# A mixture-of-experts router without the search for ties, and three ScalarE constants as immediates, in an audio tower on one core

## The chip, the core and the metric

The kernel runs on one core of a Trainium2 chip. A core has TensorE (PE: matmuls, and PEld, its weight loads), VectorE (DVE), ScalarE (ACT), GpSimd (POOL) and SyncE (SP, which issues DMAs). Each engine works through its own list of instructions in order, and the engines wait for each other by semaphores. The metric is device time in microseconds. Three runs of the kernel before took 646.54 us in the median (645.55 to 648.94).

## The reference

The input is x, 128 sequences of 375 steps and 64 features. Three layers follow one another:

```python
for i in range(3):                        # selective state-space layers
    delta = softplus(x @ W_dbc[0] * W_dt + b_dt);  B, C = x @ W_dbc[1:]
    h[t] = exp(delta * A) * h[t-1] + delta * x * B;  y = sum(h * C) + D * x
    if i < 2: x = mean of neighbouring steps of y      # 375 -> 187 -> 93
h = h + attention(layernorm(h))           # 8 heads, normalized q and k, y = 0.5(q.k)^2 + q.k + 1
h = h + experts(layernorm(h))

# experts: 6 experts, the two best of each token are mixed
rh = relu(f @ router_w1 + b1)
expert_logits = softmax(rh @ router_w2 + b2)
top_w, top_i = top_k(expert_logits, 2)    # of equal values the lower index is taken
routing_weights = softmax(top_w)
expert_out = relu(relu(f @ w1 + b1) @ w2 + b2) @ w3 + b3      # all six
out = sum over the two chosen of routing_weights * expert_out
```

The change concerns `top_k` and `routing_weights`: for each token six probabilities, of which the greatest and the second are found, with weights 1/(1+e) and e/(1+e), where e is exp(second - first).

## The kernel before

The 128 sequences are worked in 16 groups of 8 (`NG = 16`, `GB = 8`). A group passes four state-space units (A and B: the halves of the first layer; C, D: the second and third), then `att` and `ffn`. Each of these is cut into steps, such as `A.z`, `att.pm30` or `ffn.top`. Which engine does a step is fixed, and the order in which an engine does the steps of all groups is written out by hand in the table `ORDER` (one list for each engine; PE's entries also name the PSUM bank). Units of some four groups are thus in work at once. A step waits through `need(g, ...)` for the steps that it depends on, through `need(..., back=1)` for readers of a buffer in the group before.

The names that matter here:

- `att.pm` (ACT, L1057): eight times a group, squares the attention scores out of PSUM with the bias 2 (tile `two_col`), 93x744 each. PE's `y` (L1366) reads them.
- `lnv` (ACT, L1021): logarithm of a layer norm's variance plus a small constant (`eps_col`), once in `att` and once in `ffn`; `rnorm` (ACT, L1047): an exponential with the bias `ln_col`.
- the router, once a group: PE's `ffn.lg` makes the logits, 93x48 (8 sequences x 6 experts) in PSUM. DVE's `route1` (L1800, L1801: `mx`, `shift`) subtracts the greatest. ACT's `prexp` (L1082) takes the exponential. DVE's `ffn.top` (L1805 to L1816) is twelve small steps, each waiting for the one before: the sum, its reciprocal, a search for the first expert at the maximum with the help of `rank` (which settles ties), the probabilities without it, their maximum, the same search again, and `diff`, the difference of the two best. ACT's `topexp`, `topln`, `toprec` (L1086, L1090, L1094) turn `diff` into weights.
- `ffn.split` (POOL, L919 to L933): seven steps that make the gates from the two one-hot masks `oh0`, `oh1` and cut them into three bf16 parts. PE's `gT` (L1449) transposes these when the last part, `lo`, is there; ACT's `gateT` (L1112) copies them out and PE's `g_0` to `g_2` (L1422) spread them.
- `du` (L889), `y` (L893, L896), `qe` (L911) and others are POOL's further work.
- `hidw0` to `hidw2`, `fin` (DVE, L1821, L1825), PE's `o` (L1461) and `oT` (L1468), ACT's `out` (L1120, tile `osb`) end a group. `osb` is single: each `out` waits for the store of the group before.
- `prep.flags` and `prep.again` (DVE, L1584 to L1590, L1556) with PE's `prep.flag` (L1197) between them test, after the last state-space unit, whether the whole work must be done over by a general path (`GENERAL`), which does not happen with these inputs.

## Time and profile before

| | |
|---|---|
| median of three runs | 646.54 us (645.55 to 648.94) |
| span of the profiled execution | 644.8 us; its own time is not listed apart; the runs lie 0.8 to 4.1 us above the span |
| PE, DVE, ACT, POOL busy | 572.2, 540.6, 525.0, 423.5 us |
| granted clock of TensorE, mean | 0.983 |

The page gives busy time by engine, the chain of work that ended last, and groups of equal instructions with their mean duration and the idle time ahead of them. A line number is a line of the kernel; `pm<-ring,two_col` reads: writes tile `pm`, reads `ring` (PSUM) and `two_col`. "<-" behind an idle time names what ended it.

### The profile page before, as it was taken

How to read it: one execution, taken by the hardware profiler on the slowest of the kernel's cores; microseconds unless marked ns; L12 is line 12 of the kernel's file. 1: busy time of each engine (PE TensorE's matmuls, PEld its weight loads, DVE VectorE, ACT ScalarE, POOL GpSimd, SP SyncE). 2: the span in 40 equal slices, each digit the busy share in tenths (PEclk: the TensorE clock that was granted, in tenths of full speed). 3: DMA queues.
4: the chain of work that ended last, by engine and by line, in shares of the span. 5: the costliest groups of instructions: out<-in, count | busy, mean ns of one | idle time of the engine just before them, and what ended most of it. 6: DMA issues, size and time to landing. Idle time of an engine off the chain costs nothing.

```text
span 644.8 us, 22886 instructions
## 1 busy us (share of the span) xinstructions
PE 572.2 (89%) x9531; PEld 302.5 (47%) x9531; DVE 540.6 (84%) x1019; ACT 525.0 (81%) x1044; POOL 423.5 (66%) x549
## 2 busy tenths in 40 slices
PE   3777778999999999999999999999999999999972
PEld 2333234545455555455445455455545545545431
DVE  5898999999899899989898999999898987764441
ACT  1345668989899999998898998999999888888761
POOL 7758899788867677768567766767686755423110
PEclk9998879999999999999999999999999999999998
DMA  3432222221220213230211212220221001000001
GB/s 78 83 82 63 65 59 59 61 52 31 52 48 20 56 43 77 47 74 14 69 31 45 55 44 61 58 47 15 68 49 29 5 8 31 17 14 14 2 14 29
DMA packets 77575, 28.52 MB, mean 44 GB/s; under 512 B 69271, under 2 KB 77463, under 8 KB 77463
## 3 DMA queue, kind: packets, MB, share of 16 engines
q1 hardware_dynamic: 71290, 25.92, 17.6%
q10 hardware_dynamic: 6173, 1.05, 0.9%
q8 instruction: 77, 1.26, 0.9%
q14 instruction: 35, 0.29, 0.1%
HBM read 13.25 MB, written 3.05 MB: 25 GB/s over the span
## 4 chain that ended last, share of the span: by engine, by line
PE 44%; ACT 19%; DVE 17%; POOL 9%; issue 5%; DMA 2%; ACTq 2%; SPq 1%; POOLq 0%; DVEq 0%
PE ring L1274 7%; PE ring L1353 5%; ACT pm L1057 5%; PE ring L1366 4%; PE ring L1461 4%; DVE ring L1714 3%; PE ring L1260 3%; PE ring L1432 2%; PE ring L1441 2%; ACT hid L1100 2%; PE ring L1229 2%; PE ring L1249 2%; PE ring L1336 1%; PE ring L1412 1%; DVE carry_C L1710 1%
## 5 line engine op out<-in xcount | busy, mean ns | idle before, releaser
L1057 ACT ACTIVATE pm<-ring,two_col 93x744 f32<-93x744 f32 x128 | 107.4, 873 | 10.0 <-PE ring L1353 9.0
L1353 PE MATMUL ring<-q_exp,qk 32*93 32x372 f32 x512 | 56.4, 507 | 7.7 <-ACT ln_rows_a L1021 1.1
L1821 DVE TENSOR_TENSOR hidw<-hid,ring 128x744 f32<-128x744 f32 x48 | 44.3, 922 | 19.1 <-PE ring L1422 11.5
L911 POOL TENSOR_TENSOR q_exp<-qk,mask_q 128x1488 f32<-128x1488 f32 x16 | 42.9, 2683 | 22.2 <-DVE qk L1772 22.2
L1366 PE MATMUL ring<-pm,v 97*32 97x93 f32 x2048 | 53.7, 245 | 1.2 <-ACT pm L1057 0.4
L1100 ACT ACTIVATE hid<-ring,b_col 128x372 f32<-128x372 f32 x96 | 49.3, 568 | 1.5 <-PE ring L1441 0.9
L1366 PEld LDWEIGHTS ring<-pm,v 97*32 97x32 f32 x2048 | 42.4, 109 | 15.3 <-ACT pm L1057 3.4
L1107 ACT ACTIVATE hid<-ring,b_col 128x744 f32<-128x744 f32 x48 | 42.2, 879 | 8.9 <-PE ring L1432 6.4
L1432 PE MATMUL ring<-hid,w 64*64 64x372 f32 x384 | 40.3, 489 | 3.2 <-ACT hid L1100 2.7
L896 POOL TENSOR_TENSOR base_C<-base_C,carry_C 128x744 f32<-128x744 f32 x16 | 28.5, 1781 | 20.1 <-DVE carry_C L1723 9.5
L1441 PE MATMUL ring<-nrm_f,w 64*64 64x372 f32 x384 | 40.0, 486 | 0.2
L896 POOL TENSOR_TENSOR base_A<-base_A,carry_A 128x744 f32<-128x744 f32 x16 | 28.4, 1772 | 13.0 <-DVE carry_A L1723 12.9
L1461 PE MATMUL ring<-hidw,w 128*64 128x372 f32 x192 | 33.5, 484 | 0.0
L889 POOL TENSOR_TENSOR du_B<-delta_B,x_B 128x744 f32<-128x744 f32 x16 | 28.6, 1790 | 7.2 <-ACT delta_B L998 6.5
L889 POOL TENSOR_TENSOR du_A<-delta_A,x_A 128x744 f32<-128x744 f32 x16 | 28.6, 1788 | 5.3 <-ACT delta_A L998 5.2
L889 POOL TENSOR_TENSOR du_C<-delta_C,x_C 128x744 f32<-128x744 f32 x16 | 28.8, 1798 | 4.4 <-ACT delta_C L998 4.3
L1353 PEld LDWEIGHTS ring<-q_exp,qk 32*93 32x93 f32 x512 | 17.4, 154 | 25.8 <-POOL q_exp L911 2.8
L889 POOL TENSOR_TENSOR du_D<-delta_D,x_D 128x372 f32<-128x372 f32 x16 | 14.7, 917 | 21.4 <-ACT delta_D L998 17.8
L896 POOL TENSOR_TENSOR base_B<-base_B,carry_B 128x744 f32<-128x744 f32 x16 | 28.3, 1772 | 0.0
L1710 DVE TENSOR_TENSOR_SCAN carry_B<-dec_B,ring 128x744 f32<-128x744 f32 x16 | 27.2, 1698 | 0.3
L1710 DVE TENSOR_TENSOR_SCAN carry_A<-dec_A,ring 128x744 f32<-128x744 f32 x16 | 27.2, 1697 | 0.2
L1710 DVE TENSOR_TENSOR_SCAN carry_C<-dec_C,ring 128x744 f32<-128x744 f32 x16 | 27.1, 1694 | 0.1
(368 smaller groups left out, 1755.4 us busy)
## 6 DMA issues: line engine op xcount, KB each, us to landing
xin_A<-in_x_dram SPq DMA_DIRECT2D x62, 93.0 KB
xin_B<-in_x_dram SPq DMA_DIRECT2D x62, 93.0 KB
x_A<-x_A SPq DMA_DIRECT2D x32, 93.0 KB, 2.4
x_B<-x_B SPq DMA_DIRECT2D x32, 93.0 KB, 2.2
x_C<-x_C SPq DMA_DIRECT2D x32, 93.0 KB, 2.2
out_dram<-osb SPq DMA_DIRECT2D x15, 186.0 KB
x_D<-x_D SPq DMA_DIRECT2D x32, 46.5 KB, 2.2
w<-in_L_ffn_expert_w_dram SPq DMA_DIRECT2D x6, 48.0 KB
```

The lines of the kernel that those rows point to most:

```text
L889: g.tensor_tensor(halves(du[u][:]), halves(delta[u][:]), xs[u][:, 0::2, :], ALU.mult).then_inc(me, 1)
L896: g.tensor_tensor(base[u][:], base[u][:], carry[u][:], ALU.add).then_inc(me, 1)
L1057: a.activation(pm[q % 2][h][0:TOUT].rearrange("m a j n -> m a (j n)"), out_of(f"att.s{q}{h}", g)[0:TOUT, :, 0:COLS], ACT.Square, bias=two_ ...
L1100: ins = a.activation(hid1[:, h], out_of(f"ffn.h1_{k}", g)[:, h, 0:COLS], ACT.Relu, bias=b1_col[:, h, k:k + 1])
L1274: ins = mm(o[to:to + E, b, 0:wide], w[r:r + E, r:r + E], src[r:r + E, b, :], start=True, stop=True, tile_position=(r, to))
L1353: ins = mm(o[h][0:TOUT, b, 0:COLS], qk[r:r + 32, 1, q * TOUT:(q + 1) * TOUT], q_exp[r:r + 32, q].rearrange("p j n -> p (j n)"), start=True ...
L1366: ins = mm(o[32 * j:32 * j + 32, 0, h * TOUT:h * TOUT + TOUT], rows[:, at:at + 32], pm[q % 2][h][:, b, j, :], start=(b == 0), stop=(b == 1 ...
L1432: ins = mm(o[to:to + E, h, 0:COLS], w2[r:r + E, k, h], hid1[r:r + E, h], start=True, stop=True, tile_position=(r, to))
L1441: ins = mm(o[E * i:E * i + E, h, 0:COLS], w1[E * h:E * h + E, 2 * k + i], hn[E * h:E * h + E, :], start=True, stop=True, tile_position=(E ...
L1461: ins = mm(o[E * h:E * h + E, 0, 0:COLS], w3[:, k], hidw[k][:, h], start=False, stop=True, skip_group_check=True, tile_position=(0, E * h))
L1710: v.tensor_tensor_scan(carry[u][:], dec[u][:], b_made(u, g), 0.0, ALU.mult, ALU.add).then_inc(me, 1)
L1821: tt(hidw[k][:], hid2[:], out_of(f"ffn.g_{k}", g)[:, :, 0:COLS], ALU.mult).then_inc(me, 1)
```

## The change

- The bias columns `two_col`, `ln_col` and `eps_col` go; `pm`, `rnorm` and `lnv` take the numbers as immediates.
- `ffn.top` has six steps for the 16 groups of the main path: `sum`, `rest` (probabilities of the experts below the maximum), `rsum`, `m1`, `diff`, `oh1`. A tie now marks more than one expert in a mask.
- The first mask, `oh0`, is made by POOL in a new step `ffn.first`, which stands directly ahead of `ffn.split` in each group. Behind the split POOL adds both masks (`both`) and sums them up (`ties`) over the groups.
- Logits, probabilities and the reciprocal lie in SBUF (`logit`, `prob`, `st`) and no longer in the logits' PSUM bank, which `shift` frees in place of `diff`.
- The flag steps stand nearly last, behind `hidw1` of group 15, and also test the sum of ties. The general path keeps the search for ties.
- PE's, DVE's and POOL's lists are else the same, and ACT's and SP's are so wholly. A marker `!` that PE's list may carry is used by no entry.

On DVE, the router of group 0 before (`ring` is PSUM, `st` the small statistics, `oh` the masks):

```order
L1805 TENSOR_REDUCE st<-ring 93x8
L1806 RECIPROCAL ring<-st 93x8
L1807 SCALAR_TENSOR_TENSOR ring<-ring,rank 93x48
L1808 TENSOR_REDUCE st<-ring 93x8
L1809 TENSOR_TENSOR oh<-ring,st 93x48
L1810 SCALAR_TENSOR_TENSOR ring<-oh,ring 93x48
L1811 TENSOR_REDUCE st<-ring 93x8
L1812 TENSOR_TENSOR ring<-ring,st 93x48
L1813 TENSOR_TENSOR ring<-ring,rank 93x48
L1814 TENSOR_REDUCE st<-ring 93x8
L1815 TENSOR_TENSOR oh<-ring,st 93x48
L1816 SCALAR_TENSOR_TENSOR st<-st,ring 93x8
```

and with the change, from `mx` on, with the one foreign step (`quad_D`) that stands between `shift` and `sum` in both:

```order
L1803 TENSOR_REDUCE st<-ring 93x8
L1805 TENSOR_TENSOR logit<-ring,st 93x48
L1697 TENSOR_TENSOR quad_D<-ring,x_D 128x372
L1808 TENSOR_REDUCE st<-prob 93x8
L1810 SCALAR_TENSOR_TENSOR rest<-logit,prob 93x48
L1817 RECIPROCAL st<-st 93x8
L1819 TENSOR_REDUCE st<-rest 93x8
L1822 SCALAR_TENSOR_TENSOR st<-st 93x8
L1825 TENSOR_TENSOR oh<-rest,st 93x48
```

Twelve steps became six, and `diff` stands before the last mask. On POOL, the split of group 0 before, with the instruction ahead of it and the one behind:

```order
L885 TENSOR_TENSOR rows_three_A<-rows_left_A,rows_hi_A 128x186
L919 TENSOR_TENSOR gate<-oh,st 93x48
L921 TENSOR_TENSOR gate_rest<-oh,gate 93x48
L923 TENSOR_TENSOR gate<-gate_rest,st 93x48
L928 CAST gate_part<-gate 93x8x18
L930 TENSOR_TENSOR gate_part<-gate,gate_part 93x8x18
L931 TENSOR_TENSOR gate_rest<-gate,gate_part 93x48
L933 TENSOR_TENSOR gate_part<-gate_rest,gate_part 93x8x18
L889 TENSOR_TENSOR du_C<-delta_C,x_C 128x744
```

and with the change:

```order
L861 TENSOR_TENSOR rows_three_A<-rows_left_A,rows_hi_A 128x186
L896 TENSOR_SCALAR oh<-logit 93x48
L902 TENSOR_TENSOR gate<-oh,st 93x48
L904 TENSOR_TENSOR gate_rest<-oh,gate 93x48
L906 TENSOR_TENSOR gate<-gate_rest,st 93x48
L911 CAST gate_part<-gate 93x8x18
L913 TENSOR_TENSOR gate_part<-gate,gate_part 93x8x18
L914 TENSOR_TENSOR gate_rest<-gate,gate_part 93x48
L916 TENSOR_TENSOR gate_part<-gate_rest,gate_part 93x8x18
L917 TENSOR_TENSOR both<-oh 93x48
L919 TENSOR_TENSOR ties<-ties,both 93x48
L865 TENSOR_TENSOR du_C<-delta_C,x_C 128x744
```

One instruction came in front, two behind. On DVE, the flag steps before, between the `hidw1` of group 12 and `nrm_a` of group 15:

```order
L1821 TENSOR_TENSOR hidw<-hid,ring 128x744 x2
L1584 TENSOR_SCALAR ends<-least,decay_max 128x1 x4
L1586 TENSOR_SCALAR ends<-most 128x4
L1588 TENSOR_SCALAR ends<-ends 128x8
L1590 TENSOR_REDUCE flag_sum<-ends 128x1
L1683 MEMSET tick 1x1
L1556 TENSOR_SCALAR flag_i<-ring 1x1
L1683 MEMSET tick 1x1
L1759 TENSOR_TENSOR nrm_a<-ring,h_in 128x4x93
```

and with the change, at the end of the list, between `hidw1` and `hidw2` of group 15 (the last `fin` follows):

```order
L1837 TENSOR_TENSOR hidw<-hid,ring 128x744 x2
L1573 TENSOR_SCALAR ends<-least,decay_max 128x1 x4
L1575 TENSOR_SCALAR ends<-most 128x4
L1577 TENSOR_SCALAR ends<-ends 128x8
L1579 TENSOR_REDUCE flag_sum<-ends 128x1
L1581 TENSOR_REDUCE tie_sum<-ties 93x1
L1583 TENSOR_SCALAR tie_sum<-tie_sum 93x1
L1585 TENSOR_TENSOR flag_sum<-flag_sum,tie_sum 93x1
L1678 MEMSET tick 1x1
L1545 TENSOR_SCALAR flag_i<-ring 1x1
L1678 MEMSET tick 1x1
L1837 TENSOR_TENSOR hidw<-hid,ring 128x744
```

Three steps are new, and the wait of `flag_i` for PE now stands ahead of the last `hidw`. The diff, cut to its core (of `ORDER`, only the entries named above moved):

```diff
@@ -576,8 +552,8 @@
         PARTS = {"dve ffn.route1": ["mx", "shift"],
-                 "dve ffn.top": ["sum", "rsum", "key0", "kmax0", "oh0", "rest", "m1", "eq1", "key1", "kmax1", "oh1", "diff"],
-                 "pool ffn.split": ["w1", "w", "gate", "hi", "mid", "rest", "lo"]}
+                 "dve ffn.top": ["sum", "rest", "rsum", "m1", "diff", "oh1"],
+                 "pool ffn.split": ["w1", "w", "gate", "hi", "mid", "rest", "lo", "both", "ties"]}
         PARTS |= {f"pool {u}.three": ["left", "mid", "three"] for u in UNITS}
@@ -699,11 +677,9 @@
-        def router(g, k):
-
-            n_at = 64 * ("lg", "pr", "key", "rsum").index(k)
-            o_ = out_of("ffn.lg", g)[0:TOUT, 0]
-            return o_[:, n_at:n_at + GB] if k == "rsum" else o_[:, n_at:n_at + GB * NX].rearrange("m (b e) -> m b e", e=NX)
+        def logits_made(g):
+
+            return out_of("ffn.lg", g)[0:TOUT, 0, 0:GB * NX].rearrange("m (b e) -> m b e", e=NX)
@@ -913,11 +889,18 @@
             def experts(g_, u, s):
+                if s == "first":
+                    need(g_, "dve ffn.shift")
+                    need(g_, "pool ffn.ties", back=1)
+                    if g_ < NG:
+                        g.tensor_scalar(oh0[:], logit[:], 0.0, None, ALU.is_ge).then_inc(me, 1)
+                    else:
+                        g.memset(tick_pool[:, 0:1], 0.0).then_inc(me, 1)
                 if s == "split":
...
                     g.tensor_tensor(gate[:], oh1[:], st[:, 6, :, None].broadcast_to([TOUT, GB, NX]), ALU.mult).then_inc(me, 1)
-                    need(g_, "pool ffn.w1")
+                    need(g_, "pool ffn.w1", "pool ffn.first")
                     g.tensor_tensor(gate_rest[:], oh0[:], gate[:], ALU.add).then_inc(me, 1)
@@ -931,6 +914,9 @@
                     g.tensor_tensor(part[2], gate_rest[:][:, :, None, :].broadcast_to(wide), part[1], ALU.subtract).then_inc(me, 1)
+                    g.tensor_tensor(both[:], oh0[:], oh1[:], ALU.add).then_inc(me, 1)
+                    need(g_, "pool ffn.both")
+                    g.tensor_tensor(ties[:], ties[:], both[:], ALU.add).then_inc(me, 1)
@@ -1018,7 +1004,7 @@
                     need(g, f"pe {u}.rs", back=1)
-                    a.activation(ln_rows[w][:], out_of(f"{u}.var", g)[:, 0, 0:TOUT], ACT.Ln, bias=eps_col[:]).then_inc(me, 1)
+                    a.activation(ln_rows[w][:], out_of(f"{u}.var", g)[:, 0, 0:TOUT], ACT.Ln, bias=LN_EPS).then_inc(me, 1)
                 if s == "rstd":
@@ -1044,7 +1030,7 @@
                     need(g, "act att.lnorm")
-                    a.activation(qk_norm[:], qk_norm[:], ACT.Exp, bias=ln_col[:], scale=-0.5).then_inc(me, 1)
+                    a.activation(qk_norm[:], qk_norm[:], ACT.Exp, bias=12.0 * LN2, scale=-0.5).then_inc(me, 1)
                 if s == "v1":
@@ -1056,7 +1042,7 @@
                                  out_of(f"att.s{q}{h}", g)[0:TOUT, :, 0:COLS], ACT.Square,
-                                 bias=two_col[0:TOUT], scale=0.5 ** 0.5).then_inc(me, 1)
+                                 bias=2.0, scale=0.5 ** 0.5).then_inc(me, 1)
                 if s[:2] == "yT":
@@ -1078,8 +1064,8 @@
                     need(g, "dve ffn.shift")
-                    lg, pr = (router(g, k) for k in ("lg", "pr"))
-                    a.activation(pr, lg, ACT.Exp).then_inc(me, 1)
+                    need(g, "dve ffn.sum", "dve ffn.rest", back=1)
+                    a.activation(prob[:], logit[:], ACT.Exp).then_inc(me, 1)
                 if s == "topexp":
@@ -1588,7 +1577,13 @@
                     v.tensor_reduce(flag_sum[:], ends[:].rearrange("p k u -> p (k u)"), AX_X, ALU.add).then_inc(c, 1)
-                    dve.wait_ge(c, 7)
+                    need(g, "pool ffn.ties")
+                    v.tensor_reduce(tie_sum[:], ties[:].rearrange("m b e -> m (b e)"), AX_X, ALU.add).then_inc(c, 1)
+                    dve.wait_ge(c, 8)
+                    ts(tie_sum[:], tie_sum[:], 2.0 * GB * NG + 0.5, None, ALU.is_gt).then_inc(c, 1)
+                    dve.wait_ge(c, 9)
+                    tt(flag_sum[0:TOUT], flag_sum[0:TOUT], tie_sum[:], ALU.add).then_inc(c, 1)
+                    dve.wait_ge(c, 10)
                 if s[0] == "w":
@@ -1793,27 +1797,39 @@
-                if s in ("route1", "top"):
-                    lg, pr, key, rsum = (router(g, k) for k in ("lg", "pr", "key", "rsum"))
                 if s == "route1":
                     need(g, "pe ffn.lg")
+                    lg = logits_made(g)
                     step(v.tensor_reduce(st[:, 0], lg, AX_X, ALU.max), "mx")
-                    tt(lg, lg, spread(st[:, 0]), ALU.subtract).then_inc(me, 1)
+                    need(g, "act ffn.prexp", "dve ffn.rest", "pool ffn.first", back=1)
+                    tt(logit[:], lg, spread(st[:, 0]), ALU.subtract).then_inc(me, 1)
                 if s == "top":
                     need(g, "act ffn.prexp")
-                    need(g, "pool ffn.w", "act ffn.topexp", back=1)
-                    step(v.tensor_reduce(st[:, 1], pr, AX_X, ALU.add), "sum")
-                    step(v.reciprocal(rsum, st[:, 1]), "rsum")
-                    step(stt(key, lg, 0.0, rank[:], ALU.is_ge, ALU.mult), "key0")
-                    step(v.tensor_reduce(st[:, 7], key, AX_X, ALU.max), "kmax0")
-                    step(tt(oh0[:], key, spread(st[:, 7]), ALU.is_equal), "oh0")
-                    step(stt(pr, oh0[:], -4.0, pr, ALU.mult, ALU.add), "rest")
-                    step(v.tensor_reduce(st[:, 4], pr, AX_X, ALU.max), "m1")
-                    step(tt(key, pr, spread(st[:, 4]), ALU.is_ge), "eq1")
-                    step(tt(key, key, rank[:], ALU.mult), "key1")
-                    step(v.tensor_reduce(st[:, 7], key, AX_X, ALU.max), "kmax1")
-                    step(tt(oh1[:], key, spread(st[:, 7]), ALU.is_equal), "oh1")
-                    stt(st[:, 5], st[:, 4], -1.0, rsum, ALU.add, ALU.mult).then_inc(me, 1)
+                    v.tensor_reduce(st[:, 1], prob[:], AX_X, ALU.add).then_inc(me, 1)
+                    if g < NG:
+                        stt(rest[:], logit[:], 0.0, prob[:], ALU.is_lt, ALU.mult).then_inc(me, 1)
+                    else:
+                        need(g, "pool ffn.w", "pool ffn.ties", back=1)
+                        chosen(g, oh0, "first", stt(key[:], logit[:], 0.0, rank[:], ALU.is_ge, ALU.mult))
+                        dve.wait_ge(sem("ties_first"), 3 * (g - NG) + 3)
+                        stt(rest[:], oh0[:], -4.0, prob[:], ALU.mult, ALU.add).then_inc(me, 1)
+                    need(g, "dve ffn.sum")
+                    v.reciprocal(st[:, 7], st[:, 1]).then_inc(me, 1)
+                    need(g, "dve ffn.rest")
+                    v.tensor_reduce(st[:, 4], rest[:], AX_X, ALU.max).then_inc(me, 1)
+                    need(g, "dve ffn.m1")
+                    need(g, "act ffn.topexp", back=1)
+                    stt(st[:, 5], st[:, 4], -1.0, st[:, 7], ALU.add, ALU.mult).then_inc(me, 1)
+                    need(g, "pool ffn.w1", "pool ffn.both", back=1)
+                    if g < NG:
+                        tt(oh1[:], rest[:], spread(st[:, 4]), ALU.is_ge).then_inc(me, 1)
+                    else:
+                        q = sem("ties_more")
+                        tt(key[:], rest[:], spread(st[:, 4]), ALU.is_ge).then_inc(q, 1)
+                        dve.wait_ge(q, g - NG + 1)
+                        chosen(g, oh1, "second", tt(key[:], key[:], rank[:], ALU.mult))
+                        dve.wait_ge(sem("ties_second"), 3 * (g - NG) + 3)
+                        v.memset(tick[:, 13:14], 0.0).then_inc(me, 1)
                 if s[:4] == "hidw":
...
                     need(g, f"pe ffn.g_{k}", f"act ffn.hid2_{k}")
```

## Rows read from the trace of the kernel before

**Rows 1.** The page: busy time and share of the span, instructions, of each engine.

```profile
PE 572.2 (89%) x9531; PEld 302.5 (47%) x9531; DVE 540.6 (84%) x1019; ACT 525.0 (81%) x1044; POOL 423.5 (66%) x549
```

**Rows 2.** One stretch: length, busy PE, PEld, DVE, ACT, POOL, clock, DMA.

```profile
144.00:608.00 464.00, 444.43 (x7836) 240.06 (x7829) 398.97 (x714) 422.43 (x856) 303.60 (x377) 1.00 0.17 39
```

**Rows 3.** The page: shares of the chain that ended last, by engine.

```profile
PE 44%; ACT 19%; DVE 17%; POOL 9%; issue 5%; DMA 2%; ACTq 2%; SPq 1%; POOLq 0%; DVEq 0%
```

**Rows 4.** The chain in order of time: start us, us, what, pieces merged.

```profile
104.61 1.65 ACT pm L1057 x2
...
574.99 0.23 ACT ln_rows_a L1021
...
601.17 1.65 ACT pm L1057 x2
```

**Rows 5.** Groups on ACT: shapes, count, busy us, mean ns, idle us before.

```profile
L1057 ACT ACTIVATE pm<-ring,two_col 93x744 f32<-93x744 f32 x128 | 107.4, 873 | 10.0 <-PE ring L1353 9.0
...
L1047 ACT ACTIVATE qk_norm<-qk_norm,ln_col 128x186 f32<-128x186 f32 x16 | 7.2, 449 | 0.1
...
L1071 ACT ACTIVATE y_rec<-y_rec 128x186 f32<-128x186 f32 x16 | 5.7, 357 | 0.2
...
L1024 ACT ACTIVATE ln_rows_f<-ln_rows_f 128x93 f32<-128x93 f32 x16 | 4.6, 289 | 0.1
...
L1082 ACT ACTIVATE ring<-ring 93x48 f32<-93x48 f32 x16 | 3.2, 198 | 1.7 <-DVE ring L1801 1.7
```

**Rows 6.** ACT in order of time: start us, us, instruction, idle and releaser.

```profile
215.50 0.41 ACT L1041 ACTIVATE qk_norm<-ring,neps_neg 128x186 f32<-128x186 f32 x1
215.80 0.33 ACT L980 ACTIVATE rows_C<-ring 128x186 f32<-128x186 f32 x1
216.01 0.43 ACT L981 ACTIVATE rows_hi_C<-ring,row_mask 128x186 bf16<-128x186 f32 x1
```

**Rows 7.** DVE and ACT in order of time, the router of group 2.

```profile
216.89 0.20 DVE L1805 TENSOR_REDUCE st<-ring 93x8 f32<-93x48 f32 x1 [0.43 <-ACT ring L1082]
...
219.54 0.16 DVE L1816 SCALAR_TENSOR_TENSOR st<-st,ring 93x8 f32<-93x8 f32 x1
...
219.73 0.21 ACT L1086 ACTIVATE st<-st 93x8 f32<-93x8 f32 x1 [0.16 <-DVE st L1816]
```

**Rows 8.** Waits: who for whom, us in total, times, longest.

```profile
POOL gate L919 <- ACT st L1086: 27.4, 3, 16.2
...
PEld ring L1449 <- POOL gate_part L933: 3.9, 7, 0.6
...
ACT st L1086 <- DVE st L1816: 3.0, 5, 1.4
```

**Rows 9.** Groups on POOL, columns as in rows 5.

```profile
L921 POOL TENSOR_TENSOR gate_rest<-oh,gate 93x48 f32<-93x48 f32 x16 | 4.5, 284 | 1.2
...
L919 POOL TENSOR_TENSOR gate<-oh,st 93x48 f32<-93x48 f32 x16 | 4.3, 268 | 27.4 <-ACT st L1086 27.4
```

**Rows 10.** The chain, columns as in rows 4, at the split of group 2.

```profile
223.03 0.23 POOL gate L919
...
225.80 2.09 POOL q_exp L911
```

**Rows 11.** In order of time: the flag at 574 us and the last group.

```profile
573.93 0.57 DVE L1584 TENSOR_SCALAR ends<-least,decay_max 128x1 f32<-128x1 f32 x4
...
576.17 0.19 PE L1197 MATMUL ring<-blk_mean,flag_sum 128*1 128x1 f32 x2
576.45 0.15 DVE L1556 TENSOR_SCALAR flag_i<-ring 1x1 int32<-1x1 f32 x1 [1.36 <-PE ring L1198]
...
631.05 0.93 DVE L1821 TENSOR_TENSOR hidw<-hid,ring 128x744 f32<-128x744 f32 x1 [1.50 <-ACT hid L1107]
...
635.05 0.68 PE L1468 MATMUL ring<-ident,fin 128*93 128x128 f32 x4 [0.65 <-DVE fin L1825]
...
636.79 0.59 ACT L1120 ACTIVATE osb<-ring 93x512 f32<-93x512 f32 x1 [5.36 <-DMA out_dram<-osb]
```

More of the change, by code:

```diff
@@ L195, in audio_tower @@
         st = sb("st", [TOUT, 8, GB])
+        logit, prob, rest, key, ties, both = (sb(n, [TOUT, GB, NX]) for n in ("logit", "prob", "rest", "key", "ties", "both"))
+        tie_sum = sb("tie_sum", [TOUT, 1])
         gate = sb("gate", [TOUT, GB, NX])
@@ L591, in audio_tower @@
         ATT_STEPS += ["pe nrow", "act nln", "act rec", "pe nb0", "dve att0", "pe nb1", "dve att1", "pe proj", "dve mid"]
-        FFN_STEPS = NORM_STEPS + ["pe rh", "act rh", "pe lg", "dve route1", "act prexp", "dve top",
+        FFN_STEPS = NORM_STEPS + ["pe rh", "act rh", "pe lg", "dve route1", "pool first", "act prexp", "dve top",
                                   "act topexp", "act topln", "act toprec", "pool split", "pe gT", "act gateT"]
@@ L605, in entries @@
             return [(w, int(g)) for w, g in (entry.split("/")[0].split(":") for entry in text.split())]
+        FIRST = {tuple(entry.split("/")[0].split(":")) for entry in ORDER["pe"].split() if entry[-1] == "!"}
         MAIN = {who: entries(ORDER[who]) for who in ORDER}
@@ L640, in audio_tower @@
             w_, g_ = step_.split(":")
-            BANK |= {(job, int(g_)): int(b) for job, b in zip(PAIRED.get(w_, (w_,)), banks_.split(","))}
+            BANK |= {(job, int(g_)): int(b) for job, b in zip(PAIRED.get(w_, (w_,)), banks_.rstrip("!").split(","))}
         BEFORE = {}
@@ L1472, in do @@
             def do(g, u, s):
+                if (f"{u}.{s}", str(g)) in FIRST:
+                    for job in PAIRED.get(f"{u}.{s}", (f"{u}.{s}",)):
+                        bank(g, job)
                 {"att": attention, "ffn": experts, "prep": prepare}.get(u, ssm)(g, u, s)
@@ L1508, in _ @@
                     v.memset(t_[half, half], val).then_inc(made, 1)
-            for t_, val in ((zero_col, 0.0), (clamp_col, CLAMP), (under_col, -UNDERFLOW),
-                            (two_col, 2.0), (ln_col, 12.0 * LN2), (eps_col, LN_EPS)):
+            for t_, val in ((zero_col, 0.0), (clamp_col, CLAMP), (under_col, -UNDERFLOW)):
                 v.memset(t_[:], val).then_inc(made, 1)
@@ L1517, in _ @@
                     v.memset(t_[E * k:E * k + E, :], by * NORM_EPS ** 2 / (1.0 if k else SCALE2)).then_inc(made, 1)
+            v.memset(ties[:], 0.0).then_inc(made, 1)
             for e in range(NX):
@@ L1786, in spread, with chosen @@
                 return col[:, :, None].broadcast_to([TOUT, GB, NX])
+            def chosen(g, to, name, made_key):
+                q, n_q = sem(f"ties_{name}"), 3 * (g - NG)
+                made_key.then_inc(q, 1)
+                dve.wait_ge(q, n_q + 1)
+                v.tensor_reduce(st[:, 0], key[:], AX_X, ALU.max).then_inc(q, 1)
+                dve.wait_ge(q, n_q + 2)
+                tt(to[:], key[:], spread(st[:, 0]), ALU.is_equal).then_inc(q, 1)
             def experts(g, u, s):
```

7 lines of the change are left out of this document (2 added, 5 removed), and 611 rows, old and new, of the table ORDER.

## The prediction

> **What bounds the kernel now.** I read the page's busy line first [rows 1]. Three engines are near full: PE 89%, DVE 84%, ACT 81%; POOL has room at 66%. The average hides a slow start and end, so the second view is the long middle alone, 144 to 608 us, in which all units and both blocks run together [rows 2]. There PE is busy 444.4 of 464 us (96%), ACT 422.4 (91%), DVE 399.0 (86%), POOL 303.6 (65%). PE's idle time in the middle, 464 - 444.4 = 19.6 us, is all that faster helpers can give back there, since no matmul changes.
>
> The third view, the chain of waits, tells which helper work PE really waits for [rows 3]: PE 44%, ACT 19%, DVE 17%, POOL 9%. Piece by piece, the chain holds 36 whole `pm` activations of 128; the first and the last are in [rows 4], each merged with its neighbour. It holds 18 of the layer norms' `Ln` (L1021; one is shown) and 2 of the `rnorm` (L1047). Of the router's DVE steps it holds only two runs, group 2's at 216.9 us and group 15's near the end; of POOL's split of the gates three, in groups 2, 4 and 9. One rule makes this useful: a chain stays a path after the change, so the time saved cannot exceed what its own pieces lose, while another path may keep more of it.
>
> **ACT: constants as immediates.** 128 `pm`, 32 `Ln` and 16 `rnorm` activations lose a per-partition bias column. A pair of equal shape prices a column: 128x186 in SBUF takes 449 ns with one (L1047) and 357 without (L1071) [rows 5], 92 ns. `pm` takes 873 with its column. I take 0.09 us for each. ACT's busy time falls by 176 x 0.09 = 15.8 us. On the chain: 36 x 0.09 = 3.2 us, 18 x 0.09 = 1.6, 2 x 0.09 = 0.2; together 5.0 us.
>
> Neighbouring ACT instructions overlap by about 0.11 us, so one may ask whether a shorter instruction also shortens the pitch. Three in a row answer it: the one with a column starts at 215.50, the next, of equal width without one, at 215.80, and the third at 216.01 [rows 6]. Pitch 0.30 with a column, 0.21 without: the saving is real also behind a neighbour. The Trainium skill (ScalarE: Activation LUTs, What ACT_TABLE_LOAD costs) states that each pointer operand adds about 93 ns and that back-to-back ACTIVATEs overlap by about 93 ns; were the overlap the pointer's own read, the second of each pair would gain nothing, and the 17 `pm` and 11 `Ln` pieces of the chain that follow a neighbour directly would take 28 x 0.09 = 2.5 us from my sum. The two pitches here speak against that reading.
>
> `prexp` (48 columns, 16 times) now reads and writes SBUF; in PSUM it takes 198 ns. SBUF rows take 289 at 93 columns (L1024) and 357 at 186 (L1071) [rows 5]; on their line 48 columns take about 256. On the chain it stands 5 times: +0.3 us; bounds 0 (as today) and 5 x 0.09 = 0.5 (as at 93 columns).
>
> **DVE: six router steps for twelve.** Today the run from `sum` to `diff` takes 216.89 to 219.70 = 2.81 us, 12 steps at 0.16 to 0.21 us and some 0.04 us of wait between [rows 7]. After: sum 0.24, rest 0.25, rsum 0.24, m1 0.24, diff 0.20, oh1 0.21 = 1.38. DVE is relieved of 1.43 us a group, 23 us in all; `topexp` can start 1.6 us earlier, as `diff` is now fifth. That operands lie in SBUF for PSUM I take as free (bounds: minus 0.05 us a step by the 0.16 of the 8-wide `diff`, plus 0.05 by the 0.25 pitch). But this is mostly off the path: ACT waited for the last router step only 5 times, 3.0 us in total [rows 8]. In the first of the chain's two runs ACT had been idle only 0.16 us before `topexp` [rows 7]; its own older work is late next. I count twice that, 0.3 us; the ends are 0 and the whole 2 x 1.6 = 3.2 us. What the DVE queue gains elsewhere I count at nothing, because a queue that decided would put the router on the chain more often than twice. The logits' PSUM bank is freed some 3 us sooner, also at nothing: no wait of PE names a router step.
>
> **POOL: three more instructions a group.** `first` stands directly ahead of the split in every group and waits for `shift`, which is older than the `topexp` that the split needs; it therefore blocks nothing new, but its own time counts. POOL waited for `topexp` only 3 times (27.4 us, long ones near the end) [rows 8]; in the other 13 groups it came to the split late from its own queue, and there `first` lengthens the way to PE's transpose `gT`. A 93x48 tensor operation takes 268 or 284 ns, and the 1.2 us of idle time ahead of 16 dependent ones make 0.08 each [rows 9]: 0.35 us (bounds: 0 where POOL is early and waits anyway, 0.36 by the slower row). `both` and `ties` follow the last split step; `gT` doesn't wait for them, but the next POOL instruction does: 2 x 0.27 + 0.08 = 0.62 us. POOL gains 16 x 0.97 = 15.5 us of work. On the chain: 3 splits x 0.35 = 1.0 us, and behind the splits of groups 2 and 9 a POOL instruction that the chain runs on to (`q_exp` at 225.80 follows the split that it reached at 223.03 [rows 10]), 2 x 0.62 = 1.2. Together +2.2 us; bounds 0 and 13 x 0.97 = 12.6.
>
> **The flag at the end.** The test for ties moves seven DVE steps, a two-matmul sum and its reading to behind `hidw1` of group 15, with three new steps. DVE now waits there for PE, and behind that wait stand the last `hidw2` and `fin`, for which PE's last `o` and `oT` wait. The old block's steps ran from 573.93 until DVE's idle 1.36 us before 576.45 began, 1.16 us; from the matmul at 576.17 to the reading at 576.45 it is 0.28 [rows 11]. With 0.6 us for the three new steps (three router steps' worth), flag steps 1.76, matmul 0.3, reading and tick 0.2: DVE, free 1.50 us before 631.05, so at 629.55, comes to `hidw2` at about 631.8 in place of 631.05, 0.8 us late. `oT` ended at 635.05 + 0.68 = 635.73, while the last `osb` waited for the store before it until 636.79 [rows 11], so there are 1.0 us of cover. Cost nothing, and 0.3 us if the steps are slower by a third. The test itself ends before the last store does. Where the block stood at 574 us, DVE waited for PE again anyway; nothing.
>
> **Sum.** -5.0 (columns) +0.3 (prexp) -0.3 (router) +2.2 (POOL) +0 (tail) = -2.8 us. The profiled span of 644.8 becomes 642.0. The median of the runs shown, 646.54, lies 1.7 us above that span, what lies around it included; taken as unchanged this gives 643.7 us. Neighbouring paths may keep part of the 5.0 us, and part of DVE's relief may come through, so the case spans 641 to 646.
>
> **Rivals.**
> *The freed time pulls through (638.3).* ACT and DVE together lose 39 us of work and PE follows. For it: both stand at 86 to 91% in the middle, and 19.6 us of PE idle are there to be had. Against: the chain allows at most 5.0 + 3.2 = 8.2 us, if POOL's additions hide: 646.5 - 8.2 = 638.3.
>
> *POOL becomes the late one at `gT` (650).* PE's weight loader waited for the split's last step 7 times already, up to 0.6 us [rows 8]. If `first` delays PE in all 13 groups in which POOL comes late, 13 x 0.35 = 4.6 us, and half of the `both` and `ties` delay the next `du` or `q_exp`, 13 x 0.62 / 2 = 4.0, while ACT's 5.0 us end as waits for PE, it is 646.5 + 8.6 - 5.0 = 650.1. The mechanism is one queue, POOL's, and it decides from the point where the additions that reach PE exceed ACT's 5.0 us: six groups with the whole 0.97, or all of `first` and one `both` and `ties`. Against: POOL idles a third of the middle and can catch up.
>
> *Nothing at all (646.5).* The columns on the chain are made up by neighbouring paths and by POOL's 2.2 us; for it speaks that PE is busy 96% of the middle, against it that `pm` releases PE directly.
>
> *The busiest helper decides (623).* The Trainium skill (Perfetto Trace Analysis, Identifying the Most-Contended Engine) says to judge engines by occupancy, but PE by its weight loads. PE's loads are busy 47% here [rows 1], so by that rule DVE at 84% is the engine to relieve. As a mechanism: DVE's queue would set the pace and give all of its 23 us, 646.5 - 23 = 623.5. The chain's 17% for DVE and its two router runs speak against it.
>
> **How the numbers follow.** Forecast 0.48, freed time 0.22, POOL 0.17, nothing 0.10, DVE decides 0.03. About 0.5% (3.2 us: 643.3 to 649.8) is what a measurement of this kernel can tell from no change. Somewhat under half of the forecast (0.22) with the freed time and DVE cases makes faster 0.47; the rest of the forecast (0.26), nothing (0.10) and a third of the POOL case (0.06) make same 0.42; the rest, 0.11, is slower. The range of 638 to 649 leaves out a third of the freed-time case and the DVE case below and half of the POOL case above, under 0.2 in all.
>
> **What would show it.** Right: `pm` at 783 ns, L1047's successor at 357, the `Ln` rows at 250; six router steps in 1.4 us; `first` near 0.27 and a POOL busy time up by some 13 us; ACT down by 15 to 16 and DVE by 23; PE's busy time unchanged and its idle time in the middle down by 2 to 4 us. Wrong: `pm` unchanged at 873 (a constant kept in memory), PE waiting longer than today for the split at `gT`, or the last `osb` waiting for `oT` in place of its store. A PE idle time in the middle under 12 us would mean that the freed time pulled through.

## The result: slower, 652.83 us

| | before | with the change |
|---|---|---|
| median of four runs each | 647.12 us (645.55 to 648.94) | 652.83 us (652.14 to 654.82) |
| ratio, 95% interval | | 1.0095 (1.0075 to 1.0115) |
| span of the profiled execution | 644.8 us | 650.8 us (its own time 652.57) |
| mean granted clock of TensorE | 0.983 | 0.963 |

The forecast was 643.7 us, within 638 to 649. The profile after, first the page's busy line, answers to [rows 1]:

```profile
PE 571.5 (88%) x9531; PEld 302.7 (47%) x9531; DVE 521.8 (80%) x924; ACT 511.9 (79%) x1044; POOL 436.4 (67%) x597
```

DVE lost 18.8 us of work, ACT 13.1, POOL gained 12.9 and PE kept its own: the change does what it says, and the kernel is still 6 us longer. The groups on ACT with the constants as immediates, which answer to [rows 5] (shapes, count, busy us, mean ns, idle us before):

```profile
L1043 ACT ACTIVATE pm<-ring 93x744 f32<-93x744 f32 x128 | 95.8, 782 | 11.1 <-PE ring L1339 10.2
...
L1033 ACT ACTIVATE qk_norm<-qk_norm 128x186 f32<-128x186 f32 x16 | 5.7, 356 | 0.1
...
L1007 ACT ACTIVATE ln_rows_f<-ring 128x93 f32<-128x93 f32 x16 | 4.0, 251 | 1.0 <-PE ring L1277 0.9
...
L1068 ACT ACTIVATE prob<-logit 93x48 f32<-93x48 f32 x16 | 3.9, 241 | 2.1 <-DVE logit L1805 1.9
```

The first three are each 0.09 us shorter. The router of group 2 in order of time, which answers to [rows 7]:

```profile
222.93 0.20 DVE L1808 TENSOR_REDUCE st<-prob 93x8 f32<-93x48 f32 x1 [0.46 <-ACT prob L1068]
...
223.59 0.20 DVE L1825 TENSOR_TENSOR oh<-rest,st 93x48 f32<-93x48 f32 x1
...
225.10 0.20 ACT L1072 ACTIVATE st<-st 93x8 f32<-93x8 f32 x1
```

Six steps in 0.86 us, and ACT comes to `topexp` only 1.3 us later: its own queue is late, as said. POOL's groups [rows 9], with the added steps:

```profile
L896 POOL TENSOR_SCALAR oh<-logit 93x48 f32<-93x48 f32 x16 | 5.3, 330 | 19.4 <-DVE logit L1805 19.4
L919 POOL TENSOR_TENSOR ties<-ties,both 93x48 f32<-93x48 f32 x16 | 4.5, 282 | 1.3
...
L917 POOL TENSOR_TENSOR both<-oh 93x48 f32<-93x48 f32 x16 | 4.5, 281 | 0.0
```

The waits at the gates [rows 8] (us in total, times, longest): PE's weight loader waits for the split's last step about as before. The profile puts another 2.1 us down to `both` and `ties`, though `gT` in the program waits for that last step alone.

```profile
POOL gate L902 <- ACT st L1072: 4.9, 3, 2.6
...
PEld ring L1435 <- POOL gate_part L916: 3.6, 7, 0.8
...
PEld ring L1435 <- POOL both L917: 1.2, 2, 0.6
...
PEld ring L1435 <- POOL ties L919: 0.9, 2, 0.6
```

The end [rows 11]: the flag's reading, the last `hidw`, PE's `oT` and ACT's `osb`.

```profile
636.12 0.15 DVE L1545 TENSOR_SCALAR flag_i<-ring 1x1 int32<-1x1 f32 x1 [0.33 <-PE ring L1184]
636.21 0.91 DVE L1837 TENSOR_TENSOR hidw<-hid,ring 128x744 f32<-128x744 f32 x1
...
641.84 0.68 PE L1454 MATMUL ring<-ident,fin 128*93 128x128 f32 x4 [0.65 <-DVE fin L1841]
642.66 0.59 ACT L1106 ACTIVATE osb<-ring 93x512 f32<-93x512 f32 x1 [6.20 <-DMA out_dram<-osb]
```

The last `osb` still waits for the store, by 0.1 us: `oT` ends at 642.52. So where are the 6 us? Stretches of the profile show it: length; busy us (count) of PE, PEld, DVE, ACT, POOL; granted clock; DMA share; GB/s. First the kernel before, then after; its second row answers to [rows 2].

```profile
0.00:110.00 110.00, 75.35 (x844) 36.63 (x845) 97.03 (x232) 56.18 (x95) 88.00 (x129) 0.92 0.33 71
```

```profile
0.00:110.00 110.00, 70.46 (x778) 33.79 (x778) 95.11 (x225) 52.36 (x90) 83.94 (x127) 0.84 0.34 69
144.00:608.00 464.00, 441.49 (x7793) 238.77 (x7789) 380.31 (x611) 410.60 (x853) 318.18 (x423) 1.00 0.18 40
```

After 110 us PE has done 778 matmuls in place of 844, before the first router step has run. The starts of the same instructions, read from the traces of before, of the change, and of two runs below:

| start, us | before | after | input tiles moved (e11) | columns kept (e14) |
|---|---|---|---|---|
| first matmul | 10.45 | 11.49 | 11.68 | 10.47 |
| third `x_A` on ACT | 64.09 | 67.43 | 67.58 | 64.81 |
| ninth `x_A` | 239.70 | 246.58 | 245.70 | 240.25 |
| last `gateT` | 625.33 | 630.36 | 631.04 | 624.64 |

3.3 us are lost by 67 us, 6.9 by 247 us; then the changed kernel wins back 1.9, and loses 0.8 again in the wait for the last store (6.20 for 5.36 us). Two things differ in that ramp: the transfers at the start take longer, and the granted clock is lower (0.84 for 0.92). The clock was my first suspect, a move of tiles the second: dropping three columns and adding seven tiles ahead of the gate puts every tile from `rank` to `st` 96 bytes lower in SBUF, and those from `gate` on 1088 higher.

### The profile page after: what moved, and what is told of

Read it like the earlier page. It is cut to its first block, busy times and chain, and to the rows that moved or that the text cites. A ratio compares the mean times of both kernels' runs of the same rounds, so it can differ in the third digit from the quotient of the medians.

```text
span 650.8 us, 22840 instructions
## 1 busy us (share of the span) xinstructions
PE 571.5 (88%) x9531; PEld 302.7 (47%) x9531; DVE 521.8 (80%) x924; ACT 511.9 (79%) x1044; POOL 436.4 (67%) x597
## 3 DMA queue, kind: packets, MB, share of 16 engines
q1 hardware_dynamic: 71290, 25.92, 18.4%
## 4 chain that ended last, share of the span: by engine, by line
PE 51%; DVE 18%; ACT 9%; POOL 8%; issue 5%; DMA 4%; ACTq 2%; SPq 2%; POOLq 0%; DVEq 0%
PE ring L1260 7%; PE ring L1339 5%; PE ring L1352 5%; PE ring L1447 4%; PE ring L1418 3%; PE ring L1246 3%; PE ring L1427 3%; PE ring L1235 2%; DVE ring L1709 2%; PE ring L1215 2%; DVE ring L1701 2%; PE ring L1329 2%; POOL q_exp L887 1%; PE ring L1398 1%; DVE hidw L1837 1%
## 5 line engine op out<-in xcount | busy, mean ns | idle before, releaser
L1043 ACT ACTIVATE pm<-ring 93x744 f32<-93x744 f32 x128 | 95.8, 782 | 11.1 <-PE ring L1339 10.2
L887 POOL TENSOR_TENSOR q_exp<-qk,mask_q 128x1488 f32<-128x1488 f32 x16 | 42.9, 2683 | 18.8 <-DVE qk L1767 18.8
L872 POOL TENSOR_TENSOR base_C<-base_C,carry_C 128x744 f32<-128x744 f32 x16 | 28.5, 1782 | 17.5 <-DVE carry_C L1718 10.0
L1447 PE MATMUL ring<-hidw,w 128*64 128x372 f32 x192 | 35.1, 502 | 0.0
L865 POOL TENSOR_TENSOR du_D<-delta_D,x_D 128x372 f32<-128x372 f32 x16 | 14.6, 914 | 19.6 <-ACT delta_D L984 16.2
```

The source lines that it names most:

```text
L865: g.tensor_tensor(halves(du[u][:]), halves(delta[u][:]), xs[u][:, 0::2, :], ALU.mult).then_inc(me, 1)
L872: g.tensor_tensor(base[u][:], base[u][:], carry[u][:], ALU.add).then_inc(me, 1)
L887: g.tensor_tensor(q_exp[:], qk[:, 0, :].rearrange("p (q t) -> p q t", q=NPAIR)[:, :, None, :].broadcast_to(wide), mask_q[:, None, :, None] ...
L1043: a.activation(pm[q % 2][h][0:TOUT].rearrange("m a j n -> m a (j n)"), out_of(f"att.s{q}{h}", g)[0:TOUT, :, 0:COLS], ACT.Square, bias=2.0, ...
L1447: ins = mm(o[E * h:E * h + E, 0, 0:COLS], w3[:, k], hidw[k][:, h], start=False, stop=True, skip_group_check=True, tile_position=(0, E * h))
```

## The experiments

All medians are beside runs of the kernel before on the same chip (647.5 to 647.9 us; 647.1 for `after`). Place is where the input tiles `xin_A` and `xin_B` begin, in bytes past a multiple of 256; "q1" is the share of 16 DMA engines' span that its packets took.

| run | what it is | place | us | ratio (95%) | q1 |
|---|---|---|---|---|---|
| before | | 128 | | | 17.6% |
| after | the change | 32 | 652.83 | 1.0095 (1.0075, 1.0115) | 18.4% |
| e1 | before, all tiles as in after | 32 | 653.64 | 1.0089 (1.0068, 1.0110) | 18.3% |
| e2 | after, all tiles as in before | 128 | 646.47 | 0.9981 (0.9965, 0.9997) | 17.6% |
| e10 | before, low tiles 96 bytes lower | 32 | 654.38 | 1.0101 (1.0082, 1.0121) | 18.3% |
| e14 | after, three columns kept unused | 128 | 646.01 | 0.9970 (0.9959, 0.9981) | 17.7% |
| e6 | before, all 32 higher | 160 | 649.48 | 1.0028 (1.0011, 1.0045) | 17.5% |
| e7 | before, all 64 higher | 192 | 647.92 | 1.0005 (0.9989, 1.0021) | 17.5% |
| e8 | before, input 32 higher | 160 | 647.59 | 1.0008 (0.9993, 1.0024) | 17.6% |
| e11 | before, input 160 higher | 32 | 654.81 | 1.0113 (1.0095, 1.0130) | 18.5% |
| e15 | before, input 128 higher | 0 | 647.77 | 0.9997 (0.9979, 1.0015) | 17.5% |
| e16 | before, input 224 higher | 96 | 647.60 | 0.9998 (0.9977, 1.0019) | 17.6% |
| e17 | before, input 96 higher | 224 | 654.21 | 1.0111 (1.0078, 1.0144) | 18.5% |
| e20 | after, input 32 higher | 64 | 646.77 | 0.9988 (0.9970, 1.0007) | 17.8% |
| e3 | before, immediates alone | 128 | 644.50 | 0.9953 (0.9937, 0.9969) | 17.7% |
| e13 | e2 without the immediates | 128 | 652.21 | 1.0073 (1.0046, 1.0101) | 17.5% |
| e9 | e2, no ties, flag early | 128 | 644.91 | 0.9959 (0.9943, 0.9976) | 17.6% |
| e12 | e2, flag early | 128 | 647.04 | 0.9995 (0.9981, 1.0010) | 17.5% |
| e18 | e14, ties summed on DVE | 128 | 645.63 | 0.9966 (0.9950, 0.9983) | 17.8% |
| e5 | after, flag early | 32 | 652.85 | 1.0076 (1.0054, 1.0098) | 18.4% |

### Is it the places? (e1, e2, e10, e14)

```diff
 e1 (before)                                       e10: the pad is [TOUT, 24]
-        two_col, ln_col, eps_col                  (moved behind flag_i)
+        pad = sb("pad", [TOUT, 296])              (ahead of gate)
 e2 (after)                                        e14: only the three columns, unused
+        two_col, ln_col, eps_col                  (ahead of rank, unused)
-        logit, prob, rest, key, ties, both, tie_sum   (moved behind flag_i)
```

> The kernel before, with nothing changed but where its tiles lie in SBUF: the three constant columns stand at the end of the list and an unused tile of 1184 bytes before the gate, so that every other tile has the address that it has in the changed kernel (96 bytes lower, or 1088 higher). Places theory (the new addresses slow the first transfers and, through a later start, give TensorE longer at the lower granted clock): about 651 to 653 us, first matmul near 11.5 us, more than 25 us at the lower clock before 100 us. Work theory (router or immediates make the loss): 646 to 648 us and the clock of before. Tail theory (the moved flag test makes the loss): 646 to 648 us.

> The changed kernel, with the three columns kept as unused tiles and the new router tiles at the end of the list, so that every tile that both kernels have lies where it lay before. Places theory: 643 to 647 us, first matmul near 10.5 us, about 17 us at the lower clock before 100 us. Work theory: 651 to 653 us, as the changed kernel. Tail theory: 651 to 653 us.

> The kernel before with the tiles from rank to st 96 bytes lower, as in the changed kernel, and those from gate on where they were. If the loss sits in the low tiles (input, x, weights, scan): 652 to 654 us and a third of the 256-byte packets slower than 18 ns. If it sits in the gate, hidden and output tiles: 646.5 to 648.5 us.

> The changed kernel as it is, with the three columns kept as unused tiles: the low tiles lie as before, the gate and the tiles behind it 1184 bytes higher than before. If the loss sits in the low tiles: 645.5 to 647.5 us. If in the gate, hidden and output tiles: 651 to 654 us.

The same program with other addresses, e1, has the whole loss; the changed one with the old addresses, e2, none. Both bear out the places theory (e1 lies just above the 651 to 653 expected), and the work and tail theories fall. e10 and e14 put the loss among the low tiles.

The clock fell with them as a cause. e2, expected at the clock of before, ran its first 110 us at a mean of 0.86 and lost nothing. The first 110 us of e3, which wins 0.5%, and of e5, which loses 0.8%:

```profile
0.00:110.00 110.00, 74.32 (x840) 36.10 (x840) 96.69 (x232) 55.74 (x95) 87.75 (x129) 0.86 0.32 71
```

```profile
0.00:110.00 110.00, 71.08 (x778) 34.28 (x778) 94.37 (x225) 52.40 (x90) 84.06 (x127) 0.92 0.34 69
```

e3 ran the ramp at a mean of 0.86 and lost next to nothing there (840 matmuls for 844); e5 ran it at the 0.92 of before and is 66 matmuls behind.

### Which tile, and which place? (e6, e7, e8, e11, e15, e16, e17, e20)

```diff
+        pad = sb("pad", [P, 8])         # e6: 32 bytes ahead of two_col; e7: [P, 16]
+        pad_in = sb("pad_in", [P, n])   # ahead of xin; e8: n = 8, e11: 40, e15: 32, e16: 56, e17: 24, e20: 8
         xin = {u: sb(f"xin_{u}", ...) for u in "AB"}
+        pad_x = sb("pad_x", [P, m])     # e8, e20: m = 8; the others 64 - n
```

> The kernel before with one unused tile of 32 bytes ahead of the three columns, so that every tile behind it lies 32 bytes higher: xin, x and the others that began at a multiple of 64 bytes no longer do, as in the changed kernel. If what counts is where a tile begins within 64 bytes: 652 to 654 us, 256-byte packets at a mean near 19.9 ns (17.9 before). If it was the distance of 96 bytes or the order of the tiles: 646 to 649 us.

> The same with a tile of 64 bytes: all tiles move, but each keeps its place within 64 bytes. If what counts is where a tile begins within 64 bytes: 646.5 to 648.5 us and packets at 17.9 ns. If any move of the tiles upsets the start: 651 us or more.

> The kernel before with only the two input tiles xin_A and xin_B 32 bytes off their multiple of 64 (tiles behind them move by 64 bytes). If the input transfers make the loss: 651 to 653 us, the start 1 us later, quad_A of group 0 some 4 us later. If it is the swaps of x, the weights or the engines' own access: 646 to 649 us.

The rule of 64 bytes fell: e6 lost 0.3% where 0.9% was expected, e8 nothing. e6's small loss was not followed up. The next rule was 256 bytes.

> The kernel before with the two input tiles 160 bytes higher and all behind them 256 higher, so that only the input tiles begin 32 bytes past a multiple of 256, as in the changed kernel (128 past one before). If the input transfers slow down by where their 256-byte pieces begin within 256 bytes: 651 to 654 us, packets near 19.9 ns. If another low tile is meant, or an absolute address: 646.5 to 648.5 us, packets near 18 ns.

> The kernel before with the two input tiles 128 bytes higher and all behind them 256 higher: the input tiles begin at a multiple of 256. If the lower half of each 256 bytes is the slow place: 652 to 655 us, packets near 19.9 ns. If only 32 past it is slow, or odd multiples of 32 in the lower half: 646.5 to 648.5 us, packets near 18 ns.

> The same with the input tiles 96 past a multiple of 256. If the lower half of each 256 bytes is slow, or odd multiples of 32 in the lower half: 652 to 655 us. If only 32 past it is slow: 646.5 to 648.5 us.

> The same with the input tiles 224 past a multiple of 256. If the lower half is slow, or 32 alone: 646.5 to 648.5 us. If odd multiples of 32 are slow and 160 was the exception: 652 to 655 us.

> The changed kernel with 32 unused bytes ahead of the two input tiles and 32 behind them: these begin 64 past a multiple of 256 (32 in the changed kernel), x and all behind it 64 bytes higher than there, the weights ahead stay. If a 32-byte piece is what is slow: 645.5 to 647 us, as with the columns kept (646.0), packets near 18 ns. If the lower places other than 0 and 96 are slow too, or the weights' or x's places matter in the changed kernel: 650 us or more.

e11 moves nothing but the input tiles off their place within 256 bytes and is as late as the changed kernel, with its packets' time as long as there, 18.4% (page; queue, packets, MB, share of 16 engines; before, then e11):

```profile
q1 hardware_dynamic: 71290, 25.92, 17.6%
```

```profile
q1 hardware_dynamic: 71290, 25.92, 18.5%
```

With e15 to e20 all eight multiples of 32 have been tried. None of the three rules that I had written down for e11 to e17 fits: 32 and 224 are slow (224 in one run only, e17), the six others not. The rule written down for e20, that a 32-byte piece is what is slow, came out (646.77). What the two share is that the multiples of 256 cut each 256-byte piece of input into 32 and 224 bytes; 64 and 192 is not slow, and beginning at a multiple gains nothing. In the packet records 96% of the 256-byte packets take 18 ns in before, e6 to e8, e14 to e16, e18 and e20; in after, e1, e10, e11 and e17 64 to 66% do, and nearly all others 19 to 31. The Trainium skill (DMA: Bandwidth & Descriptors, How a descriptor splits into AXI transactions) says that a read which does not start at a multiple of 256 bytes begins at the one below and pays for the unused part in steps of 32 bytes. By that, 128 would be dearer than 32; on this side, where SBUF is written, the runs say otherwise.

How 1 us of DMA becomes 6: first matmul, before and e11 (start us, us, instruction, idle before and releaser).

```profile
10.45 0.77 PE L1203 MATMUL ring<-hidw 64*128 64x128 f32 x2 [10.45 <-DMA hidw<-in_L_tok_W_dt_dram]
```

```profile
11.68 0.55 PE L1205 MATMUL ring<-hidw 64*128 64x128 f32 x1 [11.68 <-DMA hidw<-in_L_tok_W_dt_dram]
```

The weights stand in the queues behind the first input: 1.2 us. That shift then meets something else. DVE and POOL at 22 us, before and e11:

```profile
21.37 0.52 DVE L1611 TENSOR_SCALAR row_w<-row_in,blk 128x16 f32<-128x16 f32 x2
...
22.28 1.81 POOL L865 MEMSET v<- 97x2048 f32 x1
...
26.53 3.30 DVE L1611 TENSOR_SCALAR row_w<-row_in,blk 128x16 f32<-128x16 f32 x2
```

```profile
23.55 2.60 DVE L1613 TENSOR_SCALAR row_w<-row_in,blk 128x16 f32<-128x16 f32 x2
23.84 1.80 POOL L867 MEMSET v<- 97x2048 f32 x1
```

Two DVE steps, 0.52 us together, meet POOL's fill of `v` and take 2.60, and `quad_A` behind them is 4.3 us late. The kernel before pays a like meeting 5 us later: its next pair takes 3.30 at 26.53 beside POOL's `du`, in e11 1.23. So of the 4.3 us 3.3 are left at the first scan (`carry_B`, 35.66 and 39.00). Later, loads and swaps that had been in time are waited for, in e11:

```profile
PEld ring L1276 <- DMA x_B<-x_B: 2.1, 1, 2.1
...
PEld ring L1231 <- DMA xin_A<-in_x_dram: 1.7, 2, 1.4
...
PEld ring L1276 <- DMA x_D<-x_D: 1.6, 1, 1.6
```

Before, no wait for `xin_A` is listed, and x_B and x_D took 1.5 and 1.0 us. e5 escaped the meeting at 22 us (`row_w` took 0.52 there) and was late all the same, so the meeting is one form of the loss, not its cause. In e11 the lag is 1.2 us at the first matmul, 3.5 at the third `x_A` and 6.0 at the ninth; from there on it does not grow (5.7 at the last `gateT`).

### What are the parts worth? (e3, e13, e9, e12, e18, e5)

```diff
 e3: before, only
-  bias=two_col[0:TOUT] / ln_col[:] / eps_col[:]
+  bias=2.0 / 12.0 * LN2 / LN_EPS
 e13: e2 with these three lines the other way round, and the fills
 e5, e9, e12: flag and again at their old places, without
-  need(g, "pool ffn.ties") and the three steps on tie_sum
 e9 also, in POOL's split
-  both = oh0 + oh1;  ties = ties + both
 e18: these two on DVE behind oh1
+  stt(both[:], logit[:], 0.0, oh1[:], ALU.is_ge, ALU.add)
+  tt(ties[:], ties[:], both[:], ALU.add)
```

> The kernel before with the three activation constants as immediates alone; the columns and the fills that make them stay, so addresses and the start are those of before. Places theory: 642 to 645 us (36 activations to pm at 0.78 instead of 0.87 us on the chain, 18 Ln, 2 rnorm). Work theory in its form that faster ACT work upsets the clock: 650 us or more. Tail theory: 642 to 645 us.

> The changed kernel's router, ties and late flag at the old places, with the three constants read from columns as before. If the parts add up (immediates 644.5, both 646.0 to 646.5, before 647.85): 649 to 650 us, so the router itself is a loss of 1.5 to 2 us. If the router costs nothing alone and takes back the immediates' gain by using up the same slack: 647.5 to 648.2 us.

> The changed kernel at the old places, without the two POOL steps that sum ties, and with the flag block at its old place; its test of ties is left out. If the ties on POOL and the late flag are what the router pays back: 642 to 644 us (below the 644.5 of the immediates alone). If the six router steps themselves or the step first on POOL cost it: 645 to 647 us, as with the ties.

> The changed kernel at the old places with POOL summing ties but the flag block at its old place, its test of ties left out. If the late flag costs what lies between the 646.5 us with and the 644.9 us without ties and late flag: 644.5 to 645.3 us. If the two POOL steps cost it: 646 to 647 us.

> The changed kernel with the three columns kept and the sum of ties as two short steps on DVE behind oh1, instead of two on POOL; the flag block stays late. If the ties cost by their place on POOL: 644 to 645.3 us (without ties and with the early flag it was 644.9). If what is paid back is the late flag or nothing that a place explains: 645.7 to 647 us, as with the columns kept.

> The changed kernel with the flag block at its old place beside group 14 instead of before the last two steps; its test of ties is left out (POOL still sums them). Tail theory: 647 to 649 us if the whole loss hung on it. Places theory: 650 to 652 us, the gain being only the 1 to 2 us that the last store loses. Work theory: as the places theory here.

The immediates alone win 3.0 us, as the places theory said. The router with everything (e2, e14) takes 1.1 to 1.8 back, by the ratios, whose intervals overlap with e3's. Without ties and with the early flag (e9) it neither wins nor loses; its 644.91 lies just between the two expectations. No cost of the late flag is clear of noise: 1.0076 against 1.0095 (e5, after) and 0.9995 against 0.9981 (e12, e2) go opposite ways. e12 and e9 differ by the ties alone, and here the intervals are apart: the ties cost 2.1 us. e2 and e14 against e9 point the same way without being clear of it. With the ties on DVE (e18) the whole is 645.63 for 646.01, between its two expectations too and with overlapping intervals, so that their place matters stays unshown. What the ties do on POOL shows in the waits of PE's weight loader for it, in e14 and then in e9:

```profile
PEld ring L1438 <- POOL gate_part L919: 3.7, 7, 0.8
...
PEld ring L1342 <- POOL q_exp L890: 3.4, 4, 1.3
...
PEld ring L1273 <- POOL h_in L872: 3.2, 7, 0.8
...
PEld ring L1438 <- POOL both L920: 1.2, 2, 0.6
...
PEld ring L1438 <- POOL ties L922: 0.9, 2, 0.6
```

```profile
PEld ring L1435 <- POOL gate_part L919: 5.1, 9, 1.0
...
PEld ring L1339 <- POOL q_exp L890: 2.9, 4, 1.1
...
PEld ring L1270 <- POOL h_in L872: 2.0, 4, 0.7
```

Together 12.4 us with the ties and 10.0 without; PE's idle time in the middle is 21.1 and 20.1 us. In e18 the same waits are 9.5 us.

e13 missed both expectations: 652.21, where the parts would add up to 649 to 650. Its profiled run is one of its shortest (649.76; the six runs reach 652.59), so the profile does not show where the upper part goes. By the ratios the router costs 4.7 us with the columns, and the three immediates are worth 6.0 behind the new router (e2 against e13) for 3.0 behind the old: the parts do not add up. Why stays open.

No run beats e3: the immediates with the old router.

## Why the prediction was wrong, point by point

**What the change moves: the step that failed.** The sum took what lies around its terms as "unchanged". It listed the instructions that the change removes, adds and moves, but not the tiles; a declaration costs no instruction, so no term, bound or rival was there for it. It is worth 6 to 7 us (653.64 against 647.55 for e1, 654.81 against 647.85 for e11), more than the sum of all terms, and has the other sign.

**The sum without it** was -2.8 us; e14 has 0.9970, -1.9 us, and e2 0.9981, -1.2; with 646.0 and 646.5 us they lie at and just above the upper end of the forecast's 641 to 646. The columns gave less and POOL took less than forecast, so part of this nearness is luck.

**Columns.** Forecast 873 to 783 ns, measured 782; 449 to 357, measured 356; Ln 251. The Trainium skill (ScalarE: Activation LUTs, What ACT_TABLE_LOAD costs) gives about 93 ns for a pointer operand; the 91 of `pm` agree. The size on the whole was off: 5.0 us of pieces on the chain gave 3.0 (e3). The chain's pieces were a ceiling, as the prediction said of the time saved, and it then took the ceiling itself. It is a ceiling for that chain only: behind the new router the columns are worth 6.0 us (e2 against e13).

**Router steps.** Forecast 1.38 us, measured 0.86: the pitch of 0.20 to 0.25 us that I took was 0.08 to 0.23. DVE lost 18.8 us for the forecast 23, ACT 13.1 for 15 to 16. That the router's gain is off the path was right (e9 against e3).

**POOL.** `first` took 330 ns for 0.27, `both` and `ties` 0.28 each; +12.9 us busy for the forecast 13. The +2.2 us on the path, with the router's -0.3 and `prexp`'s +0.3, compare with 1.1 to 1.8 beside the immediates, and with 4.7 without them (e13). The rival named `gT` and the next `q_exp`; from before to after the weight loader's waits grew at `gT` (3.9 to 5.7 us, with what is put down to `both` and `ties`), at `q_exp` (2.8 to 3.6) and at `h_in` (2.0 to 3.1).

**The tail** was forecast right in its cost, nothing that can be told from noise, but not in its steps. The last `hidw` starts 5.72 us behind the last `gateT` before and 5.85 after: the flag makes it 0.1 us late, not 0.8. The cover of 1.0 us shrank all the same, because PE's `oT` starts 5.63 us behind that `hidw` in place of 4.00, with part of the last stretch at the lower clock (before, then after):

```profile
632.00:638.00 6.00, 3.05 (x18) 1.34 (x18) 0.55 (x1) 0.59 (x1) 0.00 (x0) 1.00 0.15 36
```

```profile
638.00:644.00 6.00, 3.86 (x16) 1.41 (x12) 0.55 (x1) 0.59 (x1) 0.00 (x0) 0.78 0.14 32
```

In e14 and e2 the last `osb` waits for `oT`, which the prediction named as a sign of being wrong:

```profile
636.83 0.59 ACT L1109 ACTIVATE osb<-ring 93x512 f32<-93x512 f32 x1 [6.09 <-PE ring L1457]
```

It does so in e1 and e11 too, with the flag early, and not in e18 and e20, with the flag late, where `oT` starts about 4.0 us behind `hidw`. So it goes with the clock and not with the flag.

**Signs.** PE's idle time in the middle was to fall by 2 to 4 us; it rose from 19.6 to 22.5. Half of the 2.9 us are PE's waits for DMA, for `x_D` at 185 us and `xin_A` at 246 us: 1.9 us in place of 0.3. That sign pointed away from the helpers, to DMA. PE's longer wait at `gT`, a sign of POOL's case, came as well.

**Likelihoods.** "Slower" had 0.11, all of it on POOL's queue. The case that came had no chance of its own.

## What to carry to other kernels

A change to the list of tiles is a change to every address behind it: compare where DMA targets begin within 256 bytes before and after, and keep a dropped tile as padding until that is settled. To tell an edit from its side effect, run the old program with the new addresses and the new program with the old ones; two runs settled what the profile's clock row only seemed to explain. What shorter instructions save on the chain of waits is a ceiling: here 3 of 5 us came.
